# Row quarters in the opening, the low-rank weights laid over 128 partitions at once, and function tables loaded by their own instruction

## The chip, the core and the metric

The kernel runs on one core of a Trainium2 chip, as one program with one launch. The metric is the device time of a run in microseconds (us). In the profile, PE is the matrix engine TensorE (PEld its weight loads), DVE is VectorE, ACT is ScalarE, POOL is GpSimd, and SP is the engine that issues most transfers; sixteen DMA engines carry them. PSUM is the memory that PE writes (eight banks of 512 fp32 columns by 128 partitions), SBUF the memory that everything else works in.

## The reference, cut to what matters

Two layers work on x, 64 samples of 32 channels by 512 columns. The change touches only how the first layer begins: a small network turns each sample's 128 conditions into a softmax over 8 experts, and the sample's own 32x32 channel mix is the weighted sum of 8 expert matrices.

```
h   = gelu(embedding @ W0 + b0); h = gelu(h @ W1 + b1)
att = softmax(h @ W2 + b2)                                   # 64 x 8
agg_w = einsum('bk,koi->boi', att, weight[..., 0])           # 64 x 32 x 32
agg_b = att @ bias_k
out = einsum('boi,bih->boh', agg_w, x) + agg_b[:, :, None]
# then x = x + ffn(out): gate, up (512 -> 1376) and down (1376 -> 512), each
# y = x @ dequantised(q) + 0.02 * (x @ A @ Bm)               # A 512 x 32, Bm 32 x 1376
# second layer: grouped convolution with a context term, then an fp8 matmul; x = x + that
```

## The kernel before, in words

The 2048 rows of x (sample, channel) form 16 groups of 128 rows (4 samples each) and 4 tiles of 512 rows. fp32 products are made from a rounded high part and a low part (names ending in _hi and _lo, type fp32r). For each tile, `condition(t)` (L600) multiplies the tile's x with `mix`, which holds for each group a 128x128 block-diagonal matrix of four samples' channel mixes; DVE adds the bias and splits the result (L1223, L1234), ACT rounds the high part (L908). Then PE multiplies with the gate and up weights, chunk by chunk of 128 of the 1376 columns (L675), adds the low-rank part from `lr_b4` (L690), and multiplies with the down weights (L660). After four tiles come the convolution and the fp8 matmul (L870). Nothing schedules the program: each engine runs its instructions as written, and semaphores order them.

The opening, up to the first L675, stands so. SP (L455) issues the loads one behind the other: the packed small inputs, the expert matrices (`cond_w`), the first x tile, `stage_lr_b`, quantised weights in a ring of eight slots (L466). PE runs three small products with filler matmuls between them (`keep_clock`, L565), turns the softmax around (L585), and makes the channel mixes of all samples with 8 matmuls whose four operand copies (high and low parts) stand on 32 partitions (L592). The result lies in one PSUM bank, the output row o = 4m + q on partition quarter q. Because `mix` wants sample b of a group on partition quarter b, 16 small copies carry the first tile's blocks (8 on ACT, L905; 8 on DVE, L1215); ACT keeps the bank in `mix_kept` (L930) and makes the other tiles' blocks from it later (L935). A bias product (L597) and four more fillers (L741) stand between the mix product and `condition(0)`.

The low-rank weights take a second way. ACT rounds `stage_lr_b` (L897), POOL subtracts to get the low part (L1135), SP stores both to DRAM as `lr_b_rows` (L480), issues four slots (L482), waits for that store (L484), and reads it back twice over into `lr_b4` (L485 to L487): the 64 rows (32 high, 32 low) of gate and up go to partitions 0 to 63 by one transfer and to 64 to 127 by another. PE waits for both (L792) before the first L690.

Of the kernel before, what the change touches and what calls it, by code (L numbers as in the profile page):

```python
# [4 lines left out]
F32 = mybir.dt.float32  # L5
# [37 lines left out]
MIX_BANK, BIAS_BANK = 5, 4  # L43
FIRST_BANK = (6, 3, 7, MIX_BANK)
# [25 lines left out]
COND_WIDTHS = (B, P, P, EXPERTS, 1, 1, EXPERTS, 1, 1)  # L70
# [5 lines left out]
OB = P // S  # L76

# [6 lines left out]
def build(nc, x, cond_pack, cond_w, cond_w_rest, bias_k, gate_q, up_q, gate_s, up_s,  # L84
          lr_a, lr_b, down_q, down_s, down_a, down_b, conv_w, ctx_w, fside, ffn_w,
          batch_mask, ident_in, turned, edges, ffn_turned, bias_row, lr_b_rows, out):
    with ExitStack() as ctx:
# [3 lines left out]
        def sem(name):  # L91
# [47 lines left out]
        pad_gate = sb("pad_gate", [P, 2 * HC * I - 4 * (S // OB) * P], F32, early)  # L139
        cond_w_sb = sb("cond_w_sb", [STACKED, S // OB * P], F32, early)  # L140
        cond_w_left = sb("cond_w_left", [STACKED, S // OB * P], F32, early)
        cond_w_hi = sb("cond_w_hi", [STACKED, S // OB * P], F32R, early)
        cond_w_parts = sb("cond_w_parts", [STACKED, S // OB, P], F32R, early)
# [5 lines left out]
        att = sb("att", [B, PARTS + PARTS // 2, EXPERTS], F32, early)  # L149
        att_hi = sb("att_hi", [STACKED, B], F32R, early)  # L150
        att_parts = sb("att_parts", [STACKED, B], F32R, early)
# [10 lines left out]
        used = 4 * (COND_COLS + 2 * B + (2 + PARTS * 3 // 2) * EXPERTS + 3 * B + 6 + S + TILE + SPARE + HC * 2 * R  # L162
# [10 lines left out]
        cond_sb, w0_sb, w1_sb, w2_sb, b0_sb, b1_sb, b2_sb, w_sign, att_sign = (  # L173
            cond_in_sb[0:rows, COND_AT[n]:COND_AT[n] + COND_WIDTHS[n]]
            for n, rows in enumerate((P, P, P, P, P, P, B, STACKED, STACKED)))
# [69 lines left out]
        mix_ready, mix_saved, mix_rest = sem("mix_ready"), sem("mix_saved"), sem("mix_rest")  # L245

        att_hi_ready, att_parts_ready, att_zero = sem("att_hi_ready"), sem("att_parts_ready"), sem("att_zero")
# [186 lines left out]
        def mix_cells(src, q, b, g0, g1):  # L434

            cells = src[q * S:(q + 1) * S, :].rearrange("p (o g b) -> p b g o", g=GROUPS, b=GB)[:, b, g0:g1]
            blocks = mix[b * S:(b + 1) * S, g0:g1, b * S:(b + 1) * S].rearrange("p g (o q) -> p q g o", q=OB)[:, q]
            return blocks, cells
# [17 lines left out]
        def _(sp):  # L456
# [105 lines left out]
        def _(pe):  # L562
# [37 lines left out]
            def condition(t):  # L600

                pe.wait_ge(x_in[t], 16)
                for c in range(HC):
                    to = FIRST_BANK[c] if t == 0 else c
                    if to == MIX_BANK:
                        pe.wait_ge(mix_saved, 1)
# [1037 lines left out]
```

## Time and profile before

| | |
|---|---|
| three runs, us | 373.22 median (373.14 to 373.66) |
| the profiled execution, us | 373.0 |
| its span, first to last instruction, us | 371.2 |
| PE busy | 361.3 us, 97% of the span |
| DVE, ACT, POOL busy | 65%, 51%, 21% |
| granted TensorE clock, mean | 0.999 |

The span is cut into pieces by instruction; what lies around it (1.8 us) belongs to no engine. An engine that is busy 97% of the span can only be relieved of work or of its few waits.

### The profile page before, as it was taken

To read this page: it belongs to the slowest core of one execution; us is meant where nothing else is said; L and a number is where in the kernel's file an instruction comes from. 1 tells how busy PE (TensorE), PEld (TensorE's weight loads), DVE (VectorE), ACT (ScalarE), POOL (GpSimd) and SP (SyncE) were. 2 spreads that over 40 slices of the span, in tenths; PEclk is the share of its full clock that TensorE was granted. 3 is DMA by queue.
4 is the path that set the end of the run, shared out by engine and by line. 5 is a ranking of instruction groups with operands and counts; after the bars stand their busy time and mean duration, and the time that the engine had idled before them with its cause. 6 is when DMAs were issued, how large, how long until landed. Compare 5 with 4: busy or idle time off the path is not lost.

```text
span 371.2 us, 5798 instructions
## 1 busy us (share of the span) xinstructions
PE 361.3 (97%) x2209; PEld 301.0 (81%) x2210; DVE 243.1 (65%) x409; ACT 190.3 (51%) x345; POOL 78.7 (21%) x68
## 2 busy tenths in 40 slices
PE   7999999999999999999999999999999999998994
PEld 3777887999888879998888789988888899997331
DVE  4949989436576664265766642737888822688995
ACT  5667797202656653035555641345667510066972
POOL 4000000021222332111422241113233221142040
PEclk9999999999999999999999999999999999999999
DMA  7997693495220000222200002326000299968288
GB/s 230 344 270 245 192 299 119 152 302 87 42 44 0 0 2 1 44 42 42 44 1 2 0 0 33 52 44 155 0 3 1 65 276 279 195 153 195 85 188 267
DMA packets 82476, 41.72 MB, mean 112 GB/s; under 512 B 52417, under 2 KB 72785, under 8 KB 82321
## 3 DMA queue, kind: packets, MB, share of 16 engines
q1 hardware_dynamic: 69072, 37.70, 37.4%
q10 hardware_dynamic: 12624, 1.82, 3.1%
q0 software_dynamic: 752, 1.84, 2.8%
q8 instruction: 17, 0.28, 0.3%
q14 instruction: 11, 0.08, 0.1%
HBM read 26.55 MB, written 14.80 MB: 111 GB/s over the span
## 4 chain that ended last, share of the span: by engine, by line
PE 93%; DVE 4%; ACT 1%; issue 1%; DVEq 0%
PE ps L675 44%; PE ps L660 25%; PE ps L690 6%; PE ps L608 4%; PE ps L710 3%; PE ps L870 3%; PE ps L666 2%; PE ps L712 2%; PE ps L850 1%; PE ps L623 1%; PE ps L568 1%; DVE v_plus L1506 1%; DVE q_fp L1525 1%; DVE amax L1383 0%; DVE v_plus L1513 0%
## 5 line engine op out<-in xcount | busy, mean ns | idle before, releaser
L660 PE MATMUL ps<-down_w,h_hi 128*128 128x288 f32 (+1 forms) x352 | 76.2, 297 | 0.0
L660 PE MATMUL ps<-down_w,h_lo 128*128 128x288 f32 (+1 forms) x352 | 74.7, 293 | 0.0
L675 PE MATMUL ps<-x_hi,gate_w 128*128 128x512 f32 (+1 forms) x176 | 69.9, 397 | 0.0
L675 PE MATMUL ps<-x_lo,gate_w 128*128 128x512 f32 (+1 forms) x176 | 69.6, 396 | 0.0
L675 PE MATMUL ps<-x_hi,up_w 128*128 128x512 f32 (+1 forms) x176 | 69.6, 396 | 0.0
L675 PE MATMUL ps<-x_lo,up_w 128*128 128x512 f32 (+1 forms) x176 | 69.3, 394 | 0.0
L1146 POOL TENSOR_TENSOR h_lo<-a_buf,h_hi 128x512 fp32r<-128x512 f32 (+1 forms) x33 | 42.7, 1295 | 90.0 <-ACT h_hi L984 90.0
L660 PEld LDWEIGHTS ps<-down_w,h_hi 128*128 128x128 f32 (+1 forms) x352 | 57.2, 189 | 1.1
L660 PEld LDWEIGHTS ps<-down_w,h_lo 128*128 128x128 f32 (+1 forms) x352 | 56.1, 188 | 0.0
L1435 DVE TENSOR_TENSOR a_buf<-a_buf,b_buf 128x512 f32<-128x512 f32 (+1 forms) x44 | 49.0, 1113 | 9.2 <-ACT a_buf L1050 8.1
L1157 POOL TENSOR_TENSOR x_nat<-y_buf,x_nat 128x512 f32<-128x512 f32 x15 | 20.8, 1385 | 117.0 <-DVE y_buf L1314 117.0
L1032 ACT ACTIVATE a_buf<-ps,gate_sc 128x512 f32<-128x512 f32 (+1 forms) x44 | 30.2, 687 | 25.3 <-POOL h_lo L1146 21.9
L1426 DVE TENSOR_TENSOR b_buf<-ps,b_buf 128x512 f32<-128x512 f32 (+1 forms) x44 | 30.2, 687 | 19.1 <-ACT b_buf L1039 14.9
L1039 ACT ACTIVATE b_buf<-ps,up_sc 128x512 f32<-128x512 f32 (+1 forms) x44 | 30.2, 687 | 21.1 <-PE ps L675 20.7
L675 PEld LDWEIGHTS ps<-x_hi,up_w 128*128 128x128 f32 (+1 forms) x176 | 32.6, 185 | 8.3
L675 PEld LDWEIGHTS ps<-x_lo,up_w 128*128 128x128 f32 (+1 forms) x176 | 32.8, 186 | 8.0
L675 PEld LDWEIGHTS ps<-x_lo,gate_w 128*128 128x128 f32 (+1 forms) x176 | 32.8, 186 | 7.8
L675 PEld LDWEIGHTS ps<-x_hi,gate_w 128*128 128x128 f32 (+1 forms) x176 | 32.7, 186 | 7.9
L1314 DVE TENSOR_TENSOR y_buf<-ps,y_buf 128x512 f32<-128x512 f32 x16 | 11.1, 692 | 39.2 <-PE ps L623 39.1
L1423 DVE TENSOR_TENSOR a_buf<-ps,a_buf 128x512 f32<-128x512 f32 (+1 forms) x44 | 30.3, 688 | 8.2 <-ACT a_buf L1032 7.3
L971 ACT ACTIVATE s<-s_sum 128x64 fp32r<-128x64 f32 x16 | 4.1, 257 | 59.8 <-DVE s_sum L1297 54.8
L984 ACT ACTIVATE h_hi<-a_buf 128x512 fp32r<-128x512 f32 (+1 forms) x44 | 27.5, 625 | 8.4 <-DVE a_buf L1435 8.3
(196 smaller groups left out, 486.5 us busy)
## 6 DMA issues: line engine op xcount, KB each, us to landing
x_nat<-in_x SPq DMA_DIRECT2D x4, 1024.0 KB, 6.9
out<-x_nat SPq DMA_DIRECT2D x15, 256.0 KB, 4.5
turned<-x_nat SPq DMA_DIRECT2D x12, 256.0 KB, 3.3
x_nat<-in_down_q SPq DMA_DIRECT2D x11, 256.0 KB, 4.0
x_nat<-in_gate_q SPq DMA_DIRECT2D x10, 256.0 KB, 6.4
x_nat<-in_up_q SPq DMA_DIRECT2D x10, 256.0 KB, 6.6
edges<-zeros SPq DMA_DIRECT2D x4, 512.0 KB, 9.3
xt_own<-turned SPq DMA_DIRECT2D x6, 256.0 KB, 3.4
```

The lines of the kernel that those rows point to most:

```text
L608: last = mm(ps[:, to, (g % TG) * P:(g % TG + 1) * P], x_nat[:, g, c * P:(c + 1) * P], mix[:, g, :], start=True, stop=True)
L660: last = mm(ps[:, 4 + 2 * (j % 2) + m, 0:HALF + R], part[0:k, ic, j * P:(j + 1) * P], down_w[0:k, ic, m, :], start=first, stop=end)
L675: last = mm(ps[0:k, bank(ic, 2 * m), :], w[:, H * ic + c * k:H * ic + (c + 1) * k], part[:, c, :], start=c == 0 and part is x1_hi, stop=c ...
L690: mm(ps[0:width(ic), bank(ic, 2 * m + 1), :], lr_b4[:, m, ic * P:ic * P + width(ic)], t4[m], start=True, stop=True).then_inc(l_mm, 1)
L984: activation(h_hi[0:k, ic, :], a_buf[0:k, ic % 2, :], copy).then_inc(h_hi_ready, 1)
L1032: activation(a_buf[0:k, ic % 2, :], ps[0:k, bank(ic, 0), :], copy, scale=gate_sc[0:k, ic:ic + 1]).then_inc(ag_ready, 1)
L1039: activation(b_buf[0:k, ic % 2, :], ps[0:k, bank(ic, 2), :], copy, scale=up_sc[0:k, ic:ic + 1]).then_inc(au_ready, 1)
L1146: nc.gpsimd.tensor_tensor(h_lo[0:k, ic, :], a_buf[0:k, ic % 2, :], plain(h_hi[0:k, ic, :]), ALU.subtract).then_inc(h_lo_ready, 1)
L1157: nc.gpsimd.tensor_tensor(x_nat[:, n, :], y_buf[:, j % 2, :], x_nat[:, n, :], ALU.add).then_inc(x2_ready, 1)
L1423: v.tensor_tensor(a, ps[0:k, bank(ic, 1), :], a, ALU.add).then_inc(g_ready, 1)
L1426: v.tensor_tensor(b, ps[0:k, bank(ic, 3), :], b, ALU.add).then_inc(u_ready, 1)
L1435: v.tensor_tensor(a, a, b, ALU.mult).then_inc(h_ready, 1)
```

## The change

It has four parts.

1. Row quarters. `cond_w` is laid out so that the four output rows of a block o stand on four partition quarters (all 128 partitions, 256 columns instead of 32 partitions by 1024). DVE gives it the sign and copies it four times along the columns while it adds the low part. The softmax is repeated 16 times, not 4, before it is turned around, and a column of ones and zeros (`att_kept`) takes the place of the zeroed part. PE makes the mixes with 32 matmuls, each on one partition quarter r and into PSUM bank r; they leave sample b on partition quarter b, once for each r. So 4 larger copies (2 on DVE, 2 on ACT) carry the first tile's blocks, and 4 more, directly behind them, the other tiles' blocks; `mix_kept` and its 16 later copies go. The four fillers ahead of `condition(0)` go.
2. DVE converts slots 0 and 1 and makes the low part of `lr_a_w` behind the first bias addition, not ahead of it; slot 2 one step later.
3. `lr_b4` is filled by one transfer for gate and one for up, each to all 128 partitions, the 64 rows read twice by a source pattern that begins with a repetition of two. POOL's subtraction waits until DVE has made the bias product's operand (`att_ready`).
4. ACT's three function tables are loaded by an instruction of their own.

```
 SP
-            for half in range(2):
-                sp.dma_start(plain(lr_b4[half * 2 * R:(half + 1) * 2 * R]),
-                             lr_b_rows.rearrange("m v r n -> (v r) m n")).then_inc(lrb_laid, 16)
+            for m in range(2):
+                sp.dma_start(plain(lr_b4[:, m, :]),
+                             lr_b_rows[m].rearrange("v r n -> (v r) n").unsqueeze(0).to_broadcast([2, 2 * R, I])
+                             ).then_inc(lrb_laid, 16)
 POOL
-            nc.gpsimd.memset(att[:, 0:PARTS // 2, :], 0.0).then_inc(att_zero, 1)
             pool.wait_ge(lrb_hi, 1)
+            pool.wait_ge(att_ready, 2)
             nc.gpsimd.tensor_tensor(lr_b_parts[:, :, 1, :], stage_lr_b[:], plain(lr_b_parts[:, :, 0, :]),
 PE
-            for o in range(S // OB):
-                last = mm(ps[:, MIX_BANK, o * B:(o + 1) * B], cond_w_parts[:, o, :], att_parts[:], start=True, stop=True)
-            last.then_inc(mix_mm, 1)
+            for o in range(OC):
+                for r in range(OB):
+                    rows = slice(r * STACKED, (r + 1) * STACKED)
+                    last = mm(ps[:, r, o * B:(o + 1) * B],
+                              cond_w_parts[rows, o].rearrange("k b i -> k (b i)"),
+                              att_parts[rows, :], start=True, stop=True)
+                    if o == OC - 1:
+                        last.then_inc(mix_mm, 1)
...
-            keep_clock(4)
             pe.wait_ge(mix_ready, 2)
             condition(0)
 ACT
             def load_table(n, func):
-                activation(stat[:, 3 + n:4 + n], ones[0:B, 0:1], func)
+                nc.scalar.preload_act_table(func)
...
-            act.wait_ge(mix_mm, 1)
+            act.wait_ge(mix_mm, OB)
             act.wait_ge(mix_zero, 1)
-            for q in range(2, OB):
-                for b in range(GB):
-                    last = activation(*mix_cells(ps[:, MIX_BANK, :], q, b, 0, TG), copy)
+            for b in range(2, GB):
+                last = activation(*mix_cells(b, 0, TG), copy)
...
+            spread_rest(2)
+            act.wait_ge(aggb_mm, 1)
+            activation(agg_b[:, 0:TILE], ps[:, BIAS_BANK, :], copy).then_inc(aggb_ready, 1)
+            spread_rest(3)
             act.wait_ge(lr_in, 16)
             activation(lr_a_w[:, :, :, 0, :], stage_lr_a[:], copy).then_inc(lra_hi, 1)
-            act.wait_ge(aggb_mm, 1)
-            activation(agg_b[:, 0:TILE], ps[:, BIAS_BANK, :], copy).then_inc(aggb_ready, 1)
-            act.wait_ge(mix_ready, 2)
-            activation(mix_kept[:], ps[:, MIX_BANK, :], copy).then_inc(mix_saved, 1)
 DVE
-            for q in range(2):
-                for b in range(GB):
-                    last = v.tensor_copy(*mix_cells(ps[:, MIX_BANK, :], q, b, 0, TG))
+            for b in range(2):
+                last = v.tensor_copy(*mix_cells(b, 0, TG))
             last.then_inc(mix_ready, 1)
+            for b in range(2):
+                v.tensor_copy(*mix_cells(b, TG, GROUPS)).then_inc(mix_rest, 1)
```

On SP, behind the loads of the opening, this stands before (x_nat is the slot ring, lr_b_parts the two parts of the low-rank weights, lr_b_rows their copy in DRAM; the shape is that of what is written):

```order
L480 DMA lr_b_rows<-lr_b_parts 128x4x344 [waits lrb_ready,lrb_hi]
L469 DMA x_nat<-in_gate_q 128x512
L469 DMA x_nat<-in_up_q 128x512
L469 DMA x_nat<-in_gate_q 128x512
L469 DMA x_nat<-in_up_q 128x512
L486 DMA lr_b4<-lr_b_rows 64x2x1376 [waits lrb_stored]
L486 DMA lr_b4<-lr_b_rows 64x2x1376
```

And now:

```order
L482 DMA lr_b_rows<-lr_b_parts 128x4x344 [waits lrb_ready,lrb_hi]
L471 DMA x_nat<-in_gate_q 128x512
L471 DMA x_nat<-in_up_q 128x512
L471 DMA x_nat<-in_gate_q 128x512
L471 DMA x_nat<-in_up_q 128x512
L488 DMA lr_b4<-lr_b_rows 128x1x1376 [waits lrb_stored]
L488 DMA lr_b4<-lr_b_rows 128x1x1376
```

The places in the queue are the same; each of the two transfers now writes 128 partitions by one row of 1376 columns, not 64 partitions by two.

On PE, from the turning of the softmax to the end of `condition(0)`, before (att_parts and cond_w_parts are the operands of the mixes, att_bias that of the bias):

```order
L586 MATMUL ps<-ident,att 32x64
L568 MATMUL ps<-warm_ones 128x512 x3
L593 MATMUL ps<-att_parts,cond_w_parts 128x64 [waits mixw_ready,att_parts_ready]
L593 MATMUL ps<-att_parts,cond_w_parts 128x64 x7
L597 MATMUL ps<-att_bias,ones 128x512 [waits att_ready]
L568 MATMUL ps<-warm_ones 128x512 x4
L608 MATMUL ps<-mix,x_nat 128x128 [waits x_in0,mix_ready]
L608 MATMUL ps<-mix,x_nat 128x128 x11
L608 MATMUL ps<-mix,x_nat 128x128 [waits mix_saved]
```

And now:

```order
L588 MATMUL ps<-ident,att 128x64
L571 MATMUL ps<-warm_ones 128x512 x3
L597 MATMUL ps<-att_parts,cond_w_parts 128x64 [waits mixw_ready,att_parts_ready]
L597 MATMUL ps<-att_parts,cond_w_parts 128x64 x31
L604 MATMUL ps<-att_bias,ones 128x512 [waits att_ready]
L615 MATMUL ps<-mix,x_nat 128x128 [waits x_in0,mix_ready]
L615 MATMUL ps<-mix,x_nat 128x128 x11
L615 MATMUL ps<-mix,x_nat 128x128 [waits mix_rest]
```

24 matmuls are added ahead of the bias product, four fillers are gone behind it, and the last quarter of `condition(0)` waits for the other tiles' blocks (`mix_rest`), since it writes a bank from which they are copied.

## Rows read from the trace of the kernel before

**Rows 1.** The page: engines, and the chain that ended last by line
```profile
PE 361.3 (97%) x2209; PEld 301.0 (81%) x2210; DVE 243.1 (65%) x409; ACT 190.3 (51%) x345; POOL 78.7 (21%) x68
...
PE 93%; DVE 4%; ACT 1%; issue 1%; DVEq 0%
```
**Rows 2.** The chain in order of time, opening: start us, us, what
```profile
8.80 1.36 DVE att_bias L1208
10.16 0.04 issue
10.20 1.12 PE ps L597 x2
11.33 0.86 PE ps L568 x4
12.19 3.57 PE ps L608 x32
15.76 0.47 PE ps L675 x2
```
**Rows 3.** Timeline of PE: start us, us, instruction, [idle before, releaser]
```profile
1.63 1.89 PE L568 MATMUL ps<-warm_ones 128*128 128x512 bf16 x4 [1.63 <-DVE warm_ones L1179]
...
5.67 1.47 PE L568 MATMUL ps<-warm_ones 128*128 128x512 bf16 x6
...
8.70 1.07 PE L593 MATMUL ps<-att_parts,cond_w_parts 32*128 32x64 f32 x8
...
27.22 0.39 PE L690 MATMUL ps<-h_hi,lr_b 128*128 128x512 f32 x1
...
344.44 1.04 PE L870 MATMUL ps<-mix,q_fp 32*128 32x512 bf16 x16 [0.42 <-DVE q_fp L1528]
```
**Rows 4.** Timeline of DVE, the same columns
```profile
8.80 1.34 DVE L1208 TENSOR_TENSOR att_bias<-att_t,bias_k_sb 8x512 f32<-8x512 f32 x1
10.07 1.74 DVE L1215 COPY mix<-ps 32x32 f32<-32x32 f32 x8
...
33.80 0.69 DVE L1275 TENSOR_TENSOR ctx_rhs<-ctx_parts,stage_mask 128x512 fp32r<-128x512 f32 x1
```
**Rows 5.** Timeline of ACT, the same columns
```profile
6.71 0.20 ACT L884 ACTIVATE stat<-ones 64x1 f32<-64x1 f32 x1
6.82 0.30 ACT L895 ACTIVATE probs<-logits,stat 64x8 f32<-64x8 f32 x1
```
**Rows 6.** Timeline of POOL, the same columns
```profile
7.97 1.63 POOL L1135 TENSOR_TENSOR lr_b_parts<-stage_lr_b,lr_b_parts 128x688 fp32r<-128x688 f32 x1 [4.77 <-ACT lr_b_parts L897]
```
**Rows 7.** Timeline of SP's queue: start us, us of issuing, transfer
```profile
9.69 0.38 SPq L480 DMA_DIRECT2D lr_b_rows<-lr_b_parts  x1
...
15.58 1.33 SPq L486 DMA_DIRECT2D lr_b<-lr_b_rows  x2
```
**Rows 8.** Transfers by line: count, KB of one, us from issue to landing
```profile
cond_w_sb<-in_cond_w SPq DMA_DIRECT2D x1, 128.0 KB, 2.4
...
lr_b_rows<-lr_b_parts SPq DMA_DIRECT2D x1, 688.0 KB, 5.9
...
lr_b<-lr_b_rows SPq DMA_DIRECT2D x1, 688.0 KB, 9.7
```
**Rows 9.** Stretches: busy us of engines, granted clock, DMA share, GB/s
```profile
2.00:4.00 2.00, 2.00 (x7) 0.94 (x6) 0.00 (x0) 0.26 (x3) 1.20 (x3) 1.00 0.81 230
...
9.00:10.00 1.00, 0.77 (x7) 0.66 (x6) 1.00 (x1) 0.19 (x1) 0.60 (x1) 1.00 1.06 406
...
19.00:20.00 1.00, 1.00 (x6) 0.80 (x5) 0.00 (x0) 0.38 (x2) 0.00 (x0) 1.00 1.08 215
```
**Rows 10.** Packets of all transfers from 0 to 7 us
```profile
DMA packets 757, 1.29 MB, mean 184 GB/s; under 512 B 97, under 2 KB 353, under 8 KB 757
...
q14 instruction: 1, 0.00, 0.0%
```
**Rows 11.** One line: durations ns min/median/max, first and last start us
```profile
L978 ACT ACTIVATE t4d<-ps x16: 258/278/280, 72.8 to 319.2; 128x128 fp32r<-128x128 f32 x16
```

More of the change, by code:

```diff
@@ L138, in build @@
         early = ExitStack()
[L139 to L143, printed above, removed]
+        pad_gate = sb("pad_gate", [P, 2 * HC * I - (3 + GB) * OC * S], F32, early)
+        cond_w_sb = sb("cond_w_sb", [P, OC * S], F32, early)
+        cond_w_left = sb("cond_w_left", [P, OC * S], F32, early)
+        cond_w_hi = sb("cond_w_hi", [P, OC * S], F32R, early)
+        cond_w_parts = sb("cond_w_parts", [P, OC, GB, S], F32R, early)
         cond_in_sb = sb("cond_in_sb", [P, COND_COLS], F32, early)
@@ L148, in build @@
         probs = sb("probs", [B, EXPERTS], F32, early)
-        att = sb("att", [B, PARTS + PARTS // 2, EXPERTS], F32, early)
-        att_hi = sb("att_hi", [STACKED, B], F32R, early)
-        att_parts = sb("att_parts", [STACKED, B], F32R, early)
+        att = sb("att", [B, OB * PARTS, EXPERTS], F32, early)
+        att_hi = sb("att_hi", [P, B], F32R, early)
+        att_whole = sb("att_whole", [P, B], F32, early)
+        att_parts = sb("att_parts", [P, B], F32R, early)
         att_t = sb("att_t", [EXPERTS, B], F32, early)
@@ L171, in build @@
         early.close()
-        cond_sb, w0_sb, w1_sb, w2_sb, b0_sb, b1_sb, b2_sb, w_sign, att_sign = (
+        cond_sb, w0_sb, w1_sb, w2_sb, b0_sb, b1_sb, b2_sb, w_sign, att_sign, att_kept = (
             cond_in_sb[0:rows, COND_AT[n]:COND_AT[n] + COND_WIDTHS[n]]
-            for n, rows in enumerate((P, P, P, P, P, P, B, STACKED, STACKED)))
+            for n, rows in enumerate((P, P, P, P, P, P, B, P, P, P)))
         phase2 = ExitStack()
@@ L604, in condition @@
                     to = FIRST_BANK[c] if t == 0 else c
-                    if to == MIX_BANK:
-                        pe.wait_ge(mix_saved, 1)
+                    if t == 0 and to == BIAS_BANK - 1:
+                        pe.wait_ge(mix_rest, GB)
                     for g in range(t * TG, (t + 1) * TG):
@@ L933, in _ @@
             swap_parts(0)
-            def spread_rest(q):
-                act.wait_ge(mix_saved, 1)
-                for b in range(GB):
-                    activation(*mix_cells(mix_kept[:], q, b, TG, GROUPS), copy).then_inc(mix_rest, 1)
             def down_weights_high():
@@ L1210, in _ @@
                             ALU.mult).then_inc(att_ready, 1)
[L1211 removed]
+            dve.wait_ge(mix_mm, OB)
             dve.wait_ge(mix_zero, 1)
[L1213 to L1215 removed]
+            for b in range(2):
+                last = v.tensor_copy(*mix_cells(b, 0, TG))
             last.then_inc(mix_ready, 1)
+            for b in range(2):
+                v.tensor_copy(*mix_cells(b, TG, GROUPS)).then_inc(mix_rest, 1)
             def convert(n):
@@ L1228, in split_mixed @@
                     if c == 0 and t == 0:
+                        convert(0)
+                        convert(1)
+                        dve.wait_ge(lra_hi, 1)
+                        v.tensor_tensor(lr_a_w[:, :, :, 1, :], stage_lr_a[:], plain(lr_a_w[:, :, :, 0, :]),
+                                        ALU.subtract).then_inc(lra_ready, 1)
+                    if c == 1 and t == 0:
                         convert(2)
```

71 lines of the change are left out of this document (33 added, 38 removed).

## The prediction

> **What bounds the kernel now.** I read the page first: PE is busy 97% of the span and the chain that ended last is 93% PE [rows 1], so time comes off only where PE waits or does filler, and comes on wherever PE is made to wait. The chain in order of time then shows where that is in the opening [rows 2]: DVE makes the operand of the bias product until 10.16, PE multiplies it until 11.33, fills until 12.19, and from then on runs without a gap. So an opening that is ready earlier moves everything behind it. The next thing to read is what PE can still run into later: the first low-rank matmul starts at 27.22 [rows 3] and needs the two transfers issued at 15.58 and, 0.7 later, at about 16.3 [rows 7]; the second of them landed 9.7 after its issue, at 26.0 [rows 8]. It was 1.2 us early. That is the one transfer of the opening with so little room, and the change rewrites it.
>
> A measurement of this kernel tells no change from a change at about 0.2% (0.75 us). The profiled execution took 373.0, its span 371.2; 1.8 lie around it, and the median of the runs is 0.2 higher. I work from 373.0.
>
> **The opening, part by part.** ACT's dummy activation goes: probs started 0.11 after it [rows 5]. Against that stand the wider softmax copy and transposes and one more DVE operation (`att_whole`) between transposes and `att_parts`; each is of the size of its rows of before plus under 0.1. I set these to nothing together and start the 32 matmuls at 8.70, as the 8 did [rows 3].
>
> The 8 matmuls of one partition quarter took 1.07, that is 0.11 each and a tail [rows 3]. If 32 on four quarters overlap fully they take the same 1.07; if not at all, 32 x 0.11 + 0.16 = 3.7. The nearest row of four quarters in turn is L870: 16 matmuls of 512 columns in 1.04, where a single 512-column one on all rows takes 0.22 to 0.25, so quarters do overlap there, at about (1.04 - 0.37) / 15 = 0.045 each [rows 3]. I take 32 x 0.045 + 0.27 = 1.7: mixes ready at 10.4, not 9.77.
>
> The operand of the bias product took DVE 1.34 for 512 columns while POOL subtracted beside it (7.97 to 9.60) [rows 4, 6]; a two-operand DVE instruction of the same 512 columns with nothing beside it took 0.69 [rows 4]. POOL now waits, so I take 0.69: ready at 9.5, 0.65 earlier. PE reaches the bias product when the 32 are issued, at about 10.15, and is through with it 1.0 later, 11.1. The first tile's copies: 16 of 32 columns took 1.74 on DVE [rows 4]; two of 128 columns on each engine are 2 x 0.28 by ACT's 128-column eviction [rows 11], ready at 11.0, under the bias product. So `condition(0)` starts at 11.1 and not at 12.1: 0.9 to 1.0 gained. With full overlap it is 10.6 (1.4 gained), with none 13.2 (1.2 lost). DVE behind it: its order puts the two conversions after the first addition, but the copies for the other tiles (two of 384 columns, some 0.55 each) end before the first addition can start, and PE needs the first low part about 4.4 after it starts `condition(0)`, when DVE has just made it; a loss of up to 0.6 is possible here, no gain. The 16 later copies on ACT were off the chain.
>
> **The low-rank weights.** POOL's subtraction (1.63) now starts behind the bias operand, 9.5 and not 7.97, and ends at 11.1 [rows 6]. SP's store stands behind it, so it is issued at 11.2, not 9.69, and everything that SP has behind it moves by 1.5: four slots, which are converted ten us later and don't mind, and the two read-backs. The store landed 5.9 after its issue in a queue full of slots [rows 8]; 1.5 later that queue is emptier, and I take 5.5: the read-backs are issued at 16.7 (bounds 15.6, no loss at all, and 17.1).
>
> What they then take hangs on how many DMA engines carry them. Before, each wrote 64 partitions by two rows; while they ran the engines were fully busy but moved 215 GB/s, against 406 at 9 us [rows 9]. Now each writes 128 partitions, and its source pattern begins with a repetition of two. A transfer is handed to the engines in equal pieces of its outermost dimension. The packet count shows this for the smallest one: up to 7 us six transfers have landed, and 97 packets are under 512 bytes [rows 10]. Five transfers of 32 or 128 rows give 16 completion packets each, 80; the expert biases are 8 rows of 128 bytes, 8 data packets; one is an instruction fetch; 8 remain, so that transfer of 8 rows ran on 8 engines and not on 16. By the same cut, a source whose outermost dimension is 2 leaves two engines, whatever the destination has. The Trainium skill says this outright ("DMA: Bandwidth & Descriptors", Rules for kernel authors): a leading zero-stride broadcast of c copies confines the whole transfer to at most c engines. By it the sum is the one that follows; no run here has yet shown the case of two.
>
> Two transfers of 688 KB are 1.41 MB. An engine at its best in this trace moves 406 / 16 = 25.4 GB/s [rows 9], two of them 50.8: 27.7 us. A 128 KB transfer at an empty queue landed in 2.4 [rows 8], of which 0.3 is data at 406 GB/s; so 2.1 of start. 16.7 + 2.1 + 27.7 = 46.5. PE stands at the wait from 26.2 on (27.22 less the 1.0 gained) and goes on at 46.5: 19.3 later than before. What is late next: the slots and staging loads issued behind have their share on the same two engines and land some 3 to 5 us after; they are wanted that long after the first low-rank matmul, so I add nothing. PE has then idled 20 us. In the opening the first four filler matmuls after idling took 1.89, the last six 1.47 [rows 3]: 0.47 against 0.25 each. That fits the lower of the clock's two levels (1.2 GHz), though the granted clock is given as 1.00 there too [rows 9]. If eight matmuls at that pace come again they cost 8 x 0.22 = 1.7; between 0 and 1.7 I take 0.7.
>
> **Sum.** 373.0 + 19.3 + 0.7 = 393.0. The gain of the opening doesn't enter: PE only arrives earlier at the wait. Bounds of this case: store landing at 15.6 and no low clock, 391.2; 26 GB/s an engine and slots sharing badly, up to 397. Ends: 388.5 to 397.5.
>
> **Rivals.**
> 1. All sixteen engines carry the read-backs. For it: destination and store have 128 rows and every transfer of before that is large ran on all engines; against it, the packet count above. Then 1.41 MB into all 128 partitions at 395 to 406 GB/s is 3.5 us, landing at 16.7 + 2.1 + 3.5 = 22.3, long before 26.2, and the opening's gain stands: 373.0 - 0.9 = 372.1, faster (371.4 to 372.7 by overlap of the quarters). This is the case on the other side, and it decides from six engines upward: 1.41 MB on six is 9.2 us, landing at 28, still a small loss; on eight 6.9 us, 25.7, no wait.
> 2. As 1, but the quarters don't overlap, since weight loads of fp32r on one quarter follow each other at 0.11 [rows 3] and nothing shows them in parallel: `condition(0)` at 13.2, 374.2, slower by 0.3%. With half overlap and a late first low part the two cancel: 373.0, no change.
> 3. Two engines, and each at the slow rate that the read-backs had before, 215 / 16 = 13.4 GB/s [rows 9]: 52.5 us of data, landing at 71.3, 373.0 + 44.1 + 0.7 = 418. For it: it is the same data from the same place. Against it: two engines alone have the memory to themselves.
>
> **How the numbers follow.** Two engines at full rate 0.67; all engines and overlap 0.19; all engines without gain 0.04, with serial quarters 0.04; slow rate 0.04; the rest, 0.02, lies between. Faster 0.20, same 0.05, slower 0.75. The forecast is 393.0. Its own range is 388.5 to 397.5; because leaving out the first rival would leave out over 0.2 with the others, the range reaches down to 371.4.
>
> **What would show it.** In the chain and PE's timeline a gap of some 20 us ahead of the first low-rank matmul (L697), released by `lr_b<-lr_b_rows`, whose second landing is near 29 us; DMA share in that stretch at 2 in 16, about 0.12, and some 50 GB/s. If the landing is near 5 instead and the share near 1, rival 1 or 2 holds. The opening is read by itself: bias operand 0.69, 32 matmuls in 1.7, `condition(0)` at 11.1. A low-rank landing before 26 makes the prediction wrong, whatever the opening does.

## The result, and the profile after

The changed kernel takes 398.2 us (median of four runs, 397.5 to 398.9) against 373.3 (373.1 to 373.7): 1.0667 of the time before, 95% interval 1.0654 to 1.0680. The forecast was 393.0 and its range ended at 397.5, 0.7 below the result. The mechanism is the one forecast, and two of its terms were sized too small. The profiled execution has a span of 396.4, 25.2 more than before.

The page of the changed kernel: engines, granted clock in 40 slices of 9.9 us, and the chain by engine (answers [rows 1]).

```profile
PE 364.2 (92%) x2230; PEld 302.6 (76%) x2230; DVE 242.8 (61%) x406; ACT 183.6 (46%) x321; POOL 78.6 (20%) x67
...
PEclk9995579999999999999999999999999999999998
...
PE 85%; DMA 9%; DVE 3%; issue 1%; POOL 0%; DVEq 0%; SPq 0%; POOLq 0%
```

PE is busy 2.9 us longer than before. DMA, which had no part in the chain, now has 9% of it: the store and the read-back, one behind the other. The timeline of the changed kernel shows where (start us, us, instruction, [idle before, releaser]; answers [rows 3, 4, 6, 7]).

```profile
8.91 0.28 DVE L1205 SCALAR_TENSOR_TENSOR att_parts<-att_hi,cond_in_sb,att_whole 128x64 fp32r<-128x64 f32 x1
...
9.25 1.09 PE L597 MATMUL ps<-att_parts,cond_w_parts 32*128 32x64 f32 x32
9.35 0.68 DVE L1214 TENSOR_TENSOR att_bias<-att_t,bias_k_sb 8x512 f32<-8x512 f32 x1
10.19 1.64 POOL L1133 TENSOR_TENSOR lr_b_parts<-stage_lr_b,lr_b_parts 128x688 fp32r<-128x688 f32 x1 [7.06 <-DVE att_bias L1214]
...
11.23 3.73 PE L615 MATMUL ps<-mix,x_nat 128*128 128x128 f32 x32
...
11.92 0.38 SPq L482 DMA_DIRECT2D lr_b_rows<-lr_b_parts  x1
...
16.02 1.20 SPq L488 DMA_DIRECT2D lr_b<-lr_b_rows  x2
17.27 12.05 SPq L491 DMA_DIRECT2D down_sb<-in_down_s  x1
...
26.22 0.39 PE L682 MATMUL ps<-x_lo,gate_w 128*128 128x512 f32 x1
49.81 0.80 PE L697 MATMUL ps<-h_hi,lr_b 128*128 128x512 f32 x1 [23.20 <-DMA lr_b<-lr_b_rows]
50.41 0.63 PE L682 MATMUL ps<-x_hi,gate_w 128*128 128x512 f32 x1
...
55.38 0.39 PE L682 MATMUL ps<-x_hi,up_w 128*128 128x512 f32 x1
```

The opening is faster: `condition(0)` starts at 11.23, not 12.03. Then PE stands 23.2 us ahead of the first low-rank matmul, which starts at 49.81 and not at 27.22 [rows 3], 22.6 later. The 13 matmuls from there to 55.38 take 5.57, where 13 of 0.232 would take 3.0: 2.55 more. 22.6 + 2.55 = 25.15, the difference of the spans within 0.1. (What is left out nearly cancels: the span goes on for 4.2 behind ACT's last store, at 392.23, and for 3.9 before, and about as much was regained in between.) SP itself was stuck: the issue behind the read-backs took 12.05.

Stretches of the changed kernel (busy us of PE, PEld, DVE, ACT, POOL, then granted clock, DMA share, GB/s; answers [rows 9]):

```profile
20.00:24.00 4.00, 4.00 (x19) 3.01 (x18) 1.68 (x6) 2.16 (x4) 0.73 (x1) 1.00 0.13 54
24.00:28.00 4.00, 2.61 (x14) 1.50 (x12) 2.26 (x4) 2.72 (x5) 0.00 (x0) 1.00 0.13 54
...
36.00:40.00 4.00, 0.00 (x0) 0.00 (x0) 0.00 (x0) 0.00 (x0) 0.00 (x0) 0.50 0.60 189
...
52.00:54.00 2.00, 2.00 (x6) 1.52 (x6) 2.00 (x5) 1.24 (x4) 0.00 (x0) 0.50 0.14 52
```

A share of 0.13 is two engines of sixteen, and 54 GB/s are 27 on each. The granted clock is 0.50 (its level of 1.2 GHz) at 36 to 40, where PE idles, and still at 52 to 54, for the first matmuls behind the wait.

### The profile page after: what moved, and what is told of

Its sections match the earlier page's. It is cut to its first block, busy times and chain, and to the rows that moved or that the text cites. A ratio compares the mean times of both kernels' runs of the same rounds, so it can differ in the third digit from the quotient of the medians.

```text
span 396.4 us, 5810 instructions
## 1 busy us (share of the span) xinstructions
PE 364.2 (92%) x2230; PEld 302.6 (76%) x2230; DVE 242.8 (61%) x406; ACT 183.6 (46%) x321; POOL 78.6 (20%) x67
## 4 chain that ended last, share of the span: by engine, by line
PE 85%; DMA 9%; DVE 3%; issue 1%; POOL 0%; DVEq 0%; SPq 0%; POOLq 0%
PE ps L682 39%; PE ps L667 24%; DMA lr_b<-lr_b_rows 8%; PE ps L697 5%; PE ps L717 3%; PE ps L874 3%; PE ps L615 3%; PE ps L719 2%; PE ps L571 1%; PE ps L673 1%; PE ps L854 1%; DMA lr_b_rows<-lr_b_parts 1%; PE ps L630 1%; DVE v_plus L1514 1%; DVE q_fp L1533 1%
## 5 line engine op out<-in xcount | busy, mean ns | idle before, releaser
L1431 DVE TENSOR_TENSOR a_buf<-ps,a_buf 128x512 f32<-128x512 f32 (+1 forms) x44 | 30.3, 688 | 29.5 <-PE ps L697 24.5
L1434 DVE TENSOR_TENSOR b_buf<-ps,b_buf 128x512 f32<-128x512 f32 (+1 forms) x44 | 30.3, 688 | 23.4 <-ACT b_buf L1040 18.6
L1040 ACT ACTIVATE b_buf<-ps,up_sc 128x512 f32<-128x512 f32 (+1 forms) x44 | 30.3, 688 | 27.3 <-PE ps L682 27.1
L1051 ACT ACTIVATE a_buf<-a_buf 128x512 f32<-128x512 f32 (+1 forms) x44 | 27.5, 625 | 32.0 <-DVE a_buf L1431 31.7
L697 PE MATMUL ps<-h_hi,lr_b 128*128 128x512 f32 (+1 forms) x44 | 18.2, 414 | 23.2 <-DMA lr_b<-lr_b_rows 23.2
L1322 DVE TENSOR_TENSOR y_buf<-ps,y_buf 128x512 f32<-128x512 f32 x16 | 11.1, 692 | 39.3 <-PE ps L630 39.2
```

The source lines that it names most:

```text
L697: mm(ps[0:width(ic), bank(ic, 2 * m + 1), :], lr_b4[:, m, ic * P:ic * P + width(ic)], t4[m], start=True, stop=True).then_inc(l_mm, 1)
L1040: activation(b_buf[0:k, ic % 2, :], ps[0:k, bank(ic, 2), :], copy, scale=up_sc[0:k, ic:ic + 1]).then_inc(au_ready, 1)
L1051: activation(a_buf[0:k, ic % 2, :], a_buf[0:k, ic % 2, :], ACT.Silu).then_inc(silu_ready, 1)
L1431: v.tensor_tensor(a, ps[0:k, bank(ic, 1), :], a, ALU.add).then_inc(g_ready, 1)
L1434: v.tensor_tensor(b, ps[0:k, bank(ic, 3), :], b, ALU.add).then_inc(u_ready, 1)
```

## The experiments

"Halves" is the read-back of before, two transfers to 64 partitions each. Ratios are to the kernel before, measured beside each run, with 95% intervals; they are those of the means, the times are medians.

| run | us | ratio |
|---|---|---|
| b_repeat | 396.7 | 1.0635 (1.0617 to 1.0652) |
| a_alone | 394.6 | 1.0577 (1.0554 to 1.0599) |
| a_fill | 397.6 | 1.0655 (1.0639 to 1.0670) |
| a_halves | 376.0 | 1.0067 (1.0042 to 1.0093) |
| a_wide | 373.4 | 0.9991 (0.9974 to 1.0008) |
| a_four | 392.3 | 1.0496 (1.0457 to 1.0535) |
| a_early | 373.9 | 1.0013 (0.9998 to 1.0028) |
| b_pool | 373.1 | 0.9997 (0.9983 to 1.0011) |
| a_best | 374.4 | 1.0016 (0.9999 to 1.0032) |
| a_order | 376.5 | 1.0071 (1.0044 to 1.0097) |
| b_best | 373.9 | 1.0004 (0.9992 to 1.0015) |
| b_tables | 373.4 | 0.9993 (0.9985 to 1.0002) |
| a_direct | 372.8 | 0.9993 (0.9978 to 1.0009) |
| b_direct | 373.7 | 1.0014 (1.0005 to 1.0024) |
| a_shift | 372.5 | 0.9980 (0.9971 to 0.9988) |
| a_short | 373.7 | 1.0010 (0.9994 to 1.0026) |
| b_shift | 374.0 | 1.0016 (1.0002 to 1.0029) |
| a_last | 372.1 | 0.9963 (0.9949 to 0.9977) |

**Is it the read-back?**

```
 b_repeat: the kernel before
-                sp.dma_start(plain(lr_b4[half * 2 * R:(half + 1) * 2 * R]), ...)
+                sp.dma_start(plain(lr_b4[:, m, :]), ... .to_broadcast([2, 2 * R, I]))
 a_alone: the changed kernel, behind the read-backs
+            sp.wait_ge(lrb_laid, 2 * 16)
             sp.dma_start(down_sb[:], down_s).then_inc(down_in, 16)
 a_fill: the changed kernel
+                    keep_clock(98)
                     pe.wait_ge(lrb_laid, 2 * 16)
```

b_repeat. 

> The kernel before with only the read-back in the changed form (one transfer for gate, one for up, source pattern with a leading repetition of two). Theory 1: issued at 15.6, it lands 33.8 later as in the changed kernel, at 49.4; PE waits from 27.2 on, 22.2 us, and loses 2.4 more at the low clock: 373.3 + 24.6 = 397.9. Rival (the loss needs the other parts, above all the later store): under 390.

a_alone. 

> The changed kernel; SP waits until the two read-backs have landed before it issues the down-projection's scales and weights, the convolution's weights and the next slots. While the read-back ran alone the engines moved 54 GB/s with a busy share of 0.13, two of sixteen. Theory 2 (each of the two engines moves 27 GB/s, and a share of it goes to the transfers issued behind, which every engine must carry its part of): alone, 1.41 MB take 26.1 us from 18.1, landing at 44.2, 5.6 earlier than 49.8: 398.2 - 5.6 = 392.6. Rival 2 (the two engines move 22 GB/s of this data whatever stands behind): landing stays at 49.8, time 398 or, with late slots, more.

a_fill. 

> The changed kernel with 98 filler matmuls of 512 columns (21 to 23 us) on PE ahead of the wait for the read-back, into a bank that is free there, so that PE idles hardly at all. Theory 3 (the matmuls at 0.43 us behind the stall are PE at the clock's lower level, granted clock 0.50, and come from its idling): granted clock 1.00 throughout, the matmuls behind the wait follow each other at 0.23, and the time falls by 2.3 to 395.9. Rival 3 (they are slow from something else, data arriving late or the engine's start): no change, 398.2.

The first low-rank matmul in b_repeat, in a_alone with a stretch of its wait, and in a_fill with the fillers ahead of it:

```profile
50.11 0.80 PE L691 MATMUL ps<-h_hi,lr_b 128*128 128x512 f32 x1 [22.30 <-DMA lr_b<-lr_b_rows]
```
```profile
45.47 0.80 PE L698 MATMUL ps<-h_hi,lr_b 128*128 128x512 f32 x1 [19.28 <-DMA lr_b<-lr_b_rows]
```
```profile
36.00:40.00 4.00, 0.00 (x0) 0.00 (x0) 0.00 (x0) 0.00 (x0) 0.00 (x0) 0.50 0.13 52
```
```profile
26.84 21.33 PE L571 MATMUL ps<-warm_ones 128*128 128x512 bf16 x98
49.96 0.50 PE L697 MATMUL ps<-h_hi,lr_b 128*128 128x512 f32 x1 [1.79 <-DMA lr_b<-lr_b_rows]
50.29 0.40 PE L682 MATMUL ps<-x_hi,gate_w 128*128 128x512 f32 x1
```

The read-back alone, put into the kernel before, brings the loss (theory 1 holds): 23.4 of 24.9. Alone on the two engines it lands in 29.5 (16.0 to 45.47) at 52 to 55 GB/s all the way; with the loads behind it in the queue, in 33.8. So theory 2 holds: they took 4.3 us of the two engines' time, where 5.6 had been forecast. The issue on SP that took 12.05 in the changed kernel, and 11.05 in b_repeat, took 0.33 in a_alone, once the read-backs had landed. The forecast for the run was 392.6; the median came to 394.6, the profiled execution, the fastest of the four, to 393.8. With fillers the matmuls behind the wait follow at 0.23 and not at 0.43, and from a release 0.15 later (49.96) the span ends at 393.9, 2.5 earlier: theory 3 holds by the profile, which is of the fastest of four runs. By the medians it shows less (397.6, runs from 395.7 to 398.1, where 395.9 had been forecast), though all four runs kept a clock of 0.995 or more. A read-back that landed some 2 us later in the other three would account for it, but no trace shows that.

**How many engines, and which partitions?**

```
 a_halves: the changed kernel with the read-back of before
 a_wide: the changed kernel, lr_b_rows is (2, 2, 2, R, I), each m stored twice
+            for m in range(2):
+                for d in range(2):
+                    sp.dma_start(lr_b_rows[m, d].rearrange("v r (c n) -> (r c) v n", n=LRC), plain(lr_b_parts[:, m]))
...
+                sp.dma_start(plain(lr_b4[:, m, :]), lr_b_rows[m].rearrange("d v r n -> (d v r) n"))
 a_four: as a_wide, but (2, 2, 2, R + 1, I), the last row of each group unused: source of 4 x 32 rows
```

a_halves. 

> The changed kernel with only the read-back of the low-rank weights as it was before (two transfers, each to 64 partitions by two rows). Theory 1 (the read-back on two DMA engines is the whole loss): it is issued at 16.0 as in the changed kernel and lands 9.7 later as in the kernel before, at 25.7, half a us before PE asks for it at 26.2. No stall, and the opening's gain (first gate matmul at 14.72 and not 15.52) stands: 373.3 - 0.8 = 372.5, ratio 0.998. Rival (other parts of the change cost something too, the copies of the mixes on ACT and DVE or the later conversions): the stall goes, but the time stays above 373.3, by as much as a second gap in PE's row behind 26 us shows.

a_wide. 

> The changed kernel with the low-rank weights stored twice over in DRAM (four stores of 344 KB, where there was one of 688 KB), so that each of the two read-backs has a plain source of 128 rows, without a repetition; the destination is 128 partitions as in the changed kernel. Theory 1 (the outermost dimension of the source pattern is what is dealt out to the engines, 128 go to all sixteen): stores landed at about 18.5, read-backs issued then; 2.1 of start and 1.41 MB at 390 GB/s, 3.6, landing at 24.2, before PE asks at 26.2: 373.3 - 0.8 = 372.5. Rival a (this data moves at the 215 GB/s of the kernel before on any number of partitions): 6.6 of data, landing at 27.2 to 28.5, 374 to 375. Rival b (128 partitions at once are what is slow): landing at 45 or later, 395 and more.

a_four. 

> As a_wide, but the copies in DRAM lie in four groups of 32 rows with an unused row behind each, so that the source pattern's outermost dimension is four, without any repetition. Theory 1: four engines of 26.5 GB/s, 106 together: issued at 18.5, 2.1 and 13.3 make 33.9, and the transfers issued behind take 4 to 6 more, as they took 4.4 on two engines (49.8 against 45.4 alone): PE resumes at 38 to 40, 10.6 to 12.6 later than the 27.4 of before, and 1 to 2.4 go at the low clock: 385 to 388. Rival (only a repetition of stride zero binds a transfer to few engines): as a_wide, 372 to 375.

A stretch of a_wide with its read-backs, one of a_four, and the end of a_four's wait:

```profile
22.00:24.00 2.00, 2.00 (x10) 1.49 (x8) 1.46 (x6) 1.94 (x4) 0.73 (x1) 1.00 0.99 378
```
```profile
20.00:22.00 2.00, 2.00 (x11) 1.38 (x10) 0.34 (x2) 0.57 (x1) 0.00 (x0) 1.00 0.24 50
```
```profile
44.74 0.79 PE L697 MATMUL ps<-h_hi,lr_b 128*128 128x512 f32 x1 [18.47 <-DMA lr_b<-lr_b_rows]
```

A plain source of 128 rows runs on all engines, at 378 GB/s where 64 partitions had 215 [rows 9]. The time of a_wide, 373.4, misses its forecast of 372.5: the second read-back landed at 26.8, not 24.2, and PE waited 0.7. a_four has no repetition of stride zero and still ran on four engines (share 0.24), so it is the size of the outermost dimension that binds, as theory 1 has it. But in that stretch those four moved 50 GB/s, no more than two did, and PE went on at 44.7 and not at 38 to 40 (392.3 us, forecast 385 to 388). What each engine can write is not the whole of it. The Trainium skill has a rule that fits both this and the 215 ("SBUF — State Buffer", Door 1: The DMA port swizzle): partitions 32 apart share a port, those 64 apart do not. By it 64 partitions in a row reach half of the ports, and pieces of 32 rows, written in step, meet pairwise on one port, while two pieces of 64 do not. The traces agree (215 of 406; 50 for four engines, 54 for two); no run varied the rows' places by themselves.

a_halves, though, was 376.0 where 372.5 was expected, and theory 1's "whole loss" fell: the same read-back as before now landed late. Its chain of waits (start us, us, what):

```profile
16.57 11.40 DMA lr_b<-lr_b_rows
27.98 0.04 issue
28.02 0.50 PE ps L696
```

The second transfer took 11.4 where it took 9.7 before, and PE waited 1.9. This span (374.0) is 2.8 longer than before, but only 0.8 of that stands at the first low-rank matmul (28.02 against 27.22); 1.7 stand at the end, which came 5.6 after the issue of the last store and not 3.9. The last question below is about that part.

**What makes it late then?**

```
 a_early: a_halves without
-            pool.wait_ge(att_ready, 2)
 b_pool: the kernel before with
+            pool.wait_ge(att_ready, 2)
 a_best: a_wide with, on SP,
+            for n in range(4, RING):
+                load_slot(n)
             sp.wait_ge(lrb_hi, 1)
...
+            sp.wait_ge(lrb_laid, 2 * 16)
             sp.dma_start(down_sb[:], down_s)
 a_order: a_halves with the same order on SP
 b_best: the kernel before with a_best's SP, read-back and POOL's wait
```

a_early. 

> The changed kernel with the read-back as before (two halves) and without POOL's new wait for the bias operand, that is, of the change only the row quarters, DVE's order and the table loads. Theory 4 (in the run with halves and POOL's wait, the read-back landed at 28.0 and not at 26.0, since the store was issued 1.7 later and the four slots issued behind it stood in front of the read-backs): subtraction and store as early as before, landing near 26.0; the bias operand takes 1.34 beside POOL again, so condition(0) starts at about 11.7 and not at 11.2, PE asks at 26.7, no stall: 373.3 - 0.4 = 372.9, and the runs agree as those of before do. Rival (the larger copies or the earlier slot conversions make the read-back late): a stall of 1 to 3 at the first low-rank matmul stays, 375 to 377.

b_pool. 

> The kernel before with POOL's wait for the bias operand alone. Theory 4: the operand takes 0.68, PE starts condition(0) 0.65 earlier and asks for the low-rank weights at 26.6; but the store is issued 1.3 to 1.7 later, and the read-back lands at 27.5 to 28: a stall of 1.0 to 1.5, so 373.3 + 0.3 to 0.9 = 373.6 to 374.2, with more scatter. Rival (the read-back does not depend on it): the 0.65 is gained, 372.7.

a_best. 

> As a_wide (low-rank weights stored twice over, read back to 128 partitions from a plain source), and SP issues the four slots ahead of the stores, while it waits for POOL, not behind them, and holds the down-projection's and convolution's loads until the read-backs have landed. Theory 4 (a read-back is late by what stands in front of it and beside it): read-backs issued at about 18, landing near 24, no stall at the first low-rank matmul; the first gate matmul 0.8 to 1.3 earlier than the 15.5 of before: 372.0 to 372.6, and less scatter than a_wide. Rival (the slots or the held loads now come late somewhere else): the wait at the first low-rank matmul goes, another appears at 22 to 36 us, 373.3 or more.

a_order. 

> The same order on SP, but with one store and the two read-backs to 64 partitions each of the kernel before (packets of 5504 bytes at half the rate, 215 GB/s). Theory 4: store landed at about 16, read-backs 2.1 and 6.6 later, 24.7: no stall, 372.0 to 372.6, against 376.0 for the same read-back with the order of the changed kernel. Rival (the halves are late for another reason than the queue's order): stall as before, 375 or more.

b_best. 

> The kernel before, its opening unchanged, with the whole low-rank way of a_best: POOL's wait, stored twice, slots first, loads held. It shows what the row quarters themselves bring. Theory 5 (the row quarters bring the 0.8 by which the first gate matmul was earlier, and the low-rank way of before costs nothing): 373.0 to 373.3, that is 0.5 to 1.0 above a_best. Rival (the low-rank way of before costs something too): as a_best within 0.2.

The timeline of a_early, without POOL's wait, and a stretch of it:

```profile
8.19 1.63 POOL L1131 TENSOR_TENSOR lr_b_parts<-stage_lr_b,lr_b_parts 128x688 fp32r<-128x688 f32 x1 [5.05 <-ACT lr_b_parts L900]
...
8.38 1.51 DVE L1203 SCALAR_TENSOR_TENSOR att_parts<-att_hi,cond_in_sb,att_whole 128x64 fp32r<-128x64 f32 x1
9.95 1.08 PE L596 MATMUL ps<-att_parts,cond_w_parts 32*128 32x64 f32 x32 [1.25 <-DVE att_parts L1203]
...
11.93 5.25 PE L614 MATMUL ps<-mix,x_nat 128*128 128x128 f32 x31
```
```profile
12.00:14.00 2.00, 2.00 (x12) 2.00 (x11) 0.99 (x3) 1.72 (x4) 0.00 (x0) 0.50 1.12 347
```

The read-back landed at 26.1 (issued at 16.9, 9.2 to landing), as theory 4 has it, against 28.0 in a_halves. That PE did not wait for it says less, since PE itself came late, at 28.7. For POOL's subtraction now met the softmax's last operation: 1.51 on DVE, where it took 0.28 in the changed kernel. PE idled 1.25, and `condition(0)` ran partly at the lower clock (0.50 at 12 to 14), 5.25 for 31 matmuls instead of 3.73 for 32. That is what POOL's wait guards in the new opening. This execution is the slowest of twelve (375.4); the median, 373.9, is still 1.0 above the forecast. In b_pool the first product started at 9.17, not 8.70, so the operand's 0.65 did not show. The read-back landed about 1.1 later than before, as forecast, but PE asked later still and did not wait, and 373.1 is under the 373.6 to 374.2 of theory 4: it settles little.

The other order made things worse, and theory 4 in that form fell: a_best took 374.4 and a_order 376.5, both forecast at 372.0 to 372.6. The chain of a_best, and its GB/s from 8 to 40 us in slices of 0.8:

```profile
13.13 8.17 DMA lr_b_rows<-lr_b_parts
...
21.69 5.65 DMA lr_b<-lr_b_rows
27.34 0.04 issue
27.39 0.51 PE ps L698
```
```profile
GB/s 388 396 405 410 342 324 344 353 394 390 395 339 348 265 102 21 0 55 186 351 427 413 304 36 0 56 354 217 165 321 389 379 374 387 402 405 402 399 351 59
```

With the slots ahead, the store took 8.2 (5.6 in a_wide), and the read-back, now quick, still landed at 27.3. The engines were not full on the way: from 20 to 22 they moved next to nothing, while SP waited for the store's landing before it issued the read-back and no other load was in the queue. Store and read-back stand in series, and either order pays for that: slots behind the store fill the engines when the read-back comes (shares near 1 in a_halves and a_wide), slots ahead of it delay the store. The held loads came late besides, as the rival had it: the chain of a_best then passes through a slot's load (29.63, 5.25 long). b_best, the old opening on the same way, took 373.9. It was forecast 0.5 to 1.0 above a_best and came out 0.5 below it, so theory 5 got no support here: by this way the new opening's lead was lost again.

**What does the opening bring?**

```
 a_direct: the changed kernel; b_direct: the kernel before (PE waits for 8 * 16)
+            for v, made in enumerate((lrb_hi, lrb_ready)):
+                sp.wait_ge(made, 1)
+                for m in range(2):
+                    for d in range(2):
+                        sp.dma_start(plain(lr_b4[(2 * d + v) * R:(2 * d + v + 1) * R, m, :]).rearrange("r (c n) -> r c n", n=LRC),
+                                     plain(lr_b_parts[:, m, v, :])).then_inc(lrb_laid, 16)
 b_tables: the kernel before
-                activation(stat[:, 3 + n:4 + n], ones[0:B, 0:1], func)
+                nc.scalar.preload_act_table(func)
```

a_direct. 

> The changed kernel without the way through DRAM: the two parts of the low-rank weights are copied from SBUF to their places in SBUF by eight transfers of 172 KB (32 partitions each), the four of the high part as soon as ACT has made it, the four of the low part behind POOL's subtraction. Theory 4 (in all versions through DRAM the read-back lands at 26 to 28 since 2.1 to 2.8 MB and the slots go through full engines first, and so takes the opening's gain back at the first low-rank matmul): 1.41 MB and one latency remain, issued by 13.7, landing at 18 to 22; no stall; condition(0) at 10.7 to 11.2 against 12.0 to 12.3: 372.0 to 372.6. Rival 4 (the gain is lost elsewhere, behind the first low-rank matmul, whatever the read-back does): 373.3 or more. Rival 5 (packets of 1376 bytes into 32 partitions are slow): a stall at the first low-rank matmul.

b_direct. 

> The kernel before with the same eight transfers, its opening unchanged. Theory 4 and theory 5 (the row quarters and POOL's wait bring 0.8 to 1.0 to condition(0), and nothing in the kernel before waits for the read-back): 373.2 to 373.4, 0.7 to 1.0 above a_direct. Rival (the low-rank way of before delays something behind): 372.6 or less.

b_tables. 

> The kernel before with the function tables loaded by their own instruction alone. Step of the prediction: the dummy activation goes, 0.1 in front of the softmax's exponential, of which PE's fillers hide a part: 373.2, no change within 0.2%. Rival (loading a table without an activation delays the first use): 373.6 or more.

The chains of a_direct and b_direct: `condition(0)`, the first low-rank matmul, the last step:

```profile
10.97 3.57 PE ps L612 x32
...
26.21 0.23 PE ps L694
...
365.08 1.27 DVEq L88
```
```profile
12.35 3.57 PE ps L606 x32
...
27.54 0.23 PE ps L688
...
366.43 1.27 DVEq L87
```

Without the way through DRAM nobody waits (in a_direct the last transfer landed at about 21.7, and PE asked at 26.05), and the new opening is 1.38 ahead at `condition(0)`, 1.33 at the low-rank matmul and 1.35 at the end of the work. The medians differ by 0.9 (372.8 and 373.7), the means by 0.7. Against the kernel before, a_direct's gain is not clear of the noise (0.9978 to 1.0009), and it just missed its forecast of 372.0 to 372.6, as b_direct did its own of 373.2 to 373.4. The direct copy drops one of two transfers in series and also moves fewer bytes; no run separates the two. The tables alone change nothing (373.4), as forecast.

**Where does the rest of the 1.35 stay?** The spans of the two profiled executions differ by 0.2 only. The page's count of program fetches and the GB/s in the last 3 us (40 slices), of a_direct and of the kernel before:

```profile
q8 instruction: 18, 0.29, 0.4%
...
GB/s 410 355 410 410 437 382 382 410 355 382 301 191 28 27 55 27 27 27 27 27 27 27 27 27 27 27 27 27 0 27 0 0 0 0 0 0 0 0 0 0
```
```profile
q8 instruction: 17, 0.28, 0.3%
...
GB/s 437 383 355 355 382 382 410 382 410 383 328 301 410 410 410 410 410 382 301 355 410 410 382 410 410 410 382 246 137 0 0 0 0 0 0 0 0 0 0 0
```

In a_direct one engine, at 27 GB/s, goes on for 1.3 us behind the others. All versions with the new opening fetch program code an 18th time; a_direct does so at 365.4, among the last stores.

```
 a_shift: a_direct (t == 1); b_shift: the kernel before (t == 1 and c == 0); ahead of each such matmul on PE
+                    pe.wait_ge(const_set, 1)
+                    pe.wait_ge(const_set, 1)
 a_short: a_direct without 3 of the first 4 fillers and without the 5 behind the convolution
 a_last: a_shift, on SP between the transfers of the high and of the low part
+                    for n in range(4, RING):
+                        load_slot(n)
```

By the profile's count of instructions the two lines add one for each such matmul (5843 in b_shift, 5798 before).

a_shift. 

> The kernel of a_direct with 176 waits that are always met on PE, one ahead of each quantised matmul of the second tile, where PE's sequencer has 0.23 us for each. Theory 6: every version with the changed opening fetches program code once more than the kernel before (18 fetches of 16 KB and not 17), since its PE program is some 40 instructions longer; the last fetch falls at 365 to 367 among the last stores, and the one DMA engine that carries it ends about 1 us behind the other fifteen. Moved 176 instructions earlier, the fetch falls some 5 us earlier, ahead of the last stores: the last store issued at 366.1 lands 5.1 later, as in the versions with the opening of before, and not 5.2 plus 1: 371.7 to 372.2 against 372.8. Rival (the longer tail comes from something else, or the waits cost PE time): 372.8 or more.

a_short. 

> The kernel of a_direct with 8 filler matmuls of PE left out (three of the first four, and all five behind the convolution), 16 instructions less. Theory 6: if the end of PE's program lies less than 16 instructions behind the place that starts the 18th fetch, that fetch is gone: 17 fetches, 371.7 to 372.2. If it lies further back, nothing changes: 372.8. Rival (the fillers keep the clock up): matmuls at half pace in the opening or behind 340, 373 or more.

b_shift. 

> The kernel before with 44 such waits on PE, so that its PE program is as long as that of the changed kernel; nothing else is changed. Theory 6: an 18th fetch appears at 365 to 367, and the end is 0.4 to 1.2 later: 373.8 to 374.6. Rival: no change, 373.4.

a_last. 

> The kernel of a_shift with the four slots issued between the four transfers of the high part and the four of the low part, not behind all eight. In a_shift's profile a slot issued at 15.2 landed at 24.4 and PE waited 1.2 for what was converted from it; the low-rank weights were there 5 us before they were asked for. Theory 7 (that wait is what is left to gain): no wait of PE between 11 and 35 us, 371.8 to 372.2. Rival (the low part is now late, or the wait was of that one execution): 372.5 as before, or more.

The GB/s in the last 3 us of b_shift, of a_shift and of a_last:

```profile
GB/s 437 383 355 328 382 410 382 410 410 410 355 383 301 410 382 410 410 410 410 273 110 27 27 27 27 27 27 0 27 0 0 0 0 0 0 0 0 0 0 0
```
```profile
GB/s 383 382 410 410 437 382 355 328 355 355 410 437 437 328 328 410 382 355 410 437 410 355 328 382 382 437 164 55 27 27 0 0 0 0 0 0 0 0 0 0
```
```profile
GB/s 383 410 410 382 300 382 382 437 383 410 382 355 328 355 437 437 410 246 110 27 0 27 27 27 27 27 27 27 27 0 0 0 0 0 0 0 0 0 0 0
```

In a_shift the fetch came at 360.3, and the last store, issued by ACT at 367.39, was followed by the end 4.0 later (5.2 in a_direct, 3.9 before). Bringing an 18th fetch into the kernel before (b_shift, at 366.2) cost 0.7 by the medians (1.0002 to 1.0029), and one engine ended alone. The added waits cost PE nothing: from the second tile's `condition` to the third's it is 76.07 us in b_shift as before. In the eight profiles whose last fetch came among the last stores and took about 0.9 (the changed kernel, a_alone, a_four, a_wide, a_best, a_direct, a_short, b_shift) the span ended 5.9 to 6.0 after that fetch began, wherever the last store fell. So theory 6 holds for a fetch in that place. It is not all of the tail: in a_last, whose last fetch came at 360.1, one engine still went on alone for some 0.8 us, and the end came 4.7 after the last store; why stays open. Nor is the gain of moving the fetch clear: a_shift took 372.5 where 371.7 to 372.2 had been forecast, and its interval overlaps that of a_direct. a_short kept its 18 fetches, and without the fillers its matmuls in the opening ran at the slow pace (2.74 for six, 1.47 before): 373.7, nothing gained. The Trainium skill tells how an engine's program comes in ("Runtime: NRT & Kernel Launch", Instruction fetch mechanics): blocks of 16 KiB, 256 instructions, by a DMA, at a cost it calls "mostly hidden". The traces agree on the blocks (16 KB each); that one of them can cost 0.7 at the end is what these runs add.

a_last is the fastest version: 372.1, 0.9963 (0.9949 to 0.9977), in five runs, 0.4% below the kernel before and in the range that theory 7 gave; a_shift's interval lies below 1 too. In its profile, of the slowest of the five (373.1), the only wait for the low-rank weights is this:

```profile
26.62 0.50 PE L698 MATMUL ps<-h_hi,lr_b 128*128 128x512 f32 x1 [0.27 <-DMA lr_b<-lr_b_parts]
```

## Why the prediction was right in its mechanism, and where its size failed

- **The mechanism was right**: a source that begins with a repetition of two leaves two engines, shown by the share of 0.13, by b_repeat and by a_four. Their rate was right too: 27 GB/s each, 25.4 taken; alone they needed 29.5, forecast as 2.1 + 27.7 = 29.8. The Trainium skill's rule cited in the prediction holds here; rivals 1 and 3 fell by the trace, rival 2 by the overlap of the quarters (32 matmuls in 1.09).
- **The step that failed** is "What is late next: the slots and staging loads issued behind have their share on the same two engines and land some 3 to 5 us after; ... I add nothing." They had their share on the two engines before the read-back was through, not after it: 4.3 us (49.81 against 45.47 in a_alone). SP's issue of 12.05, which took 0.33 in a_alone, fits that. The upper bound of 397 allowed for slots that share badly, but not together with all of the low clock; the lower end of 388.5 follows from none of the terms (its own bound was 391.2).
- **The second term too small**: the lower clock, 0.7 taken with 1.7 as its bound, was 2.55: 13 matmuls were slow, not eight.
- **The store** was issued 0.7 later than forecast (11.92), since the first fillers stayed at the slow pace longer (2.07 for six, 1.47 before) and the bias operand came at 10.03, not 9.5. It landed after 4.1, not 5.5, so the read-backs were issued at 16.0, not 16.7: 0.7 gained.
- **Sum with measured sizes**: 393.0 - 0.7 (issue) - 0.3 (start and data) + 4.3 + 1.8 = 398.1, against 398.2.
- **The opening**: the bias operand took 0.68 (0.69 forecast). That `condition(0)` came at 11.23 (11.1 forecast) is luck, for two errors cancel: the 32 matmuls took 1.09, the bound of full overlap, not 1.7, and they started at 9.25, not 8.70. In a_halves, a_wide and a_direct, where they started at 8.7 to 8.8, `condition(0)` came at 10.7 to 10.8, near the 10.6 that the prediction gave for full overlap.
- **Rival 1 was probably priced too well.** On sixteen engines it was to end at 372.1, with 5.6 from the read-backs' issue to their landing. The nearest run, a_wide, took 373.4: its second read-back took 7.9 on engines that the slots kept full. a_wide also stores twice as much, so it is not the rival's own case. The rival did not see the last fetch either.

## What to carry to other kernels

Look at the outermost dimension of both patterns of a transfer before its size in bytes: here two meant two engines and four meant four, everything issued behind on that queue shared the two, and the issuing engine was held up. An earlier opening is worth what the latest transfer behind it allows: find that transfer's landing and what stands in front of it first. Here other orders of a store and a read-back in series gained nothing; a direct copy in their place kept the lead up to the last matmul. Where stores end the kernel, look at whether one DMA engine ends alone, and whether a program fetch fell among them.

## What the runs showed of the hardware that was not expected

- Four engines, in a stretch of 2 us, moved no more than two into 128 partitions (50 and 54 GB/s), and sixteen moved 378 into 128 partitions but 215 into 64.
- An issue on SP took 12.05 us behind two transfers that ran on two engines, and 0.33 once they had landed (a_alone).
- 32 fp32r matmuls on four row quarters took 1.09, eight on one quarter 1.07 [rows 3].
- A 0.28 DVE operation took 1.51 when POOL's subtraction had started 0.2 before it.
- Behind a wait of 23 us PE ran 5 us at the lower clock, behind one of 1.8 after fillers at full clock not at all.
- One more fetch of 16 KB of program code among the last stores cost 0.7 us (b_shift; 0.1 to 1.1 by its interval).
